# Two-expert outputs: weighting on ScalarE, adding on GpSimd, and a later place for the last normalisation steps

## The reference

```python
    # 2: sparse experts, two for each token
    out = out + w_e[:, None] * h
    # 3: learned adjacency, mixed with the layer norm of x
    return (1.0 - gamma) * adj_raw + gamma * A_learned
    # 4: transformer block
    h = _rmsnorm(hidden_states, ln1_w)
    q = (h @ Wq); k = (h @ Wk); v = (h @ Wv)
```

## Time and profile before

| what | value |
|---|---|
| median of 3 runs | 1102.59 us (1101.93 to 1104.66) |
| the profiled execution's own time | 1102.88 us |
| its span (what the profile covers) | 1101.0 us |
| PE busy | 1006.5 us, 91% |
| DVE busy | 868.8 us, 79% |
| ACT busy | 613.7 us, 56% |
| POOL busy | 430.9 us, 39% |

### The profile page before, as it was taken

The page is one execution under the profiler, slowest core; times in us unless marked ns, Lnnn a source line. Parts: engine busy times, 40 slices in busy tenths (PEclk is TensorE's granted clock), DMA queues, the critical chain, the costliest instruction groups (busy, mean ns, idle before and its releaser), DMA issues.

```text
span 1101.0 us, 20158 instructions
## 1 busy us (share of the span) xinstructions
PE 1006.5 (91%) x5934; PEld 821.6 (75%) x5934; DVE 868.8 (79%) x2642; ACT 613.7 (56%) x1748; POOL 430.9 (39%) x372
## 2 busy tenths in 40 slices
PE   4788877999996489999999999999998999999997
PEld 2455545466663368999999999999887888888886
DVE  6999996577773889878777877777868888788877
ACT  4789983533232377777787777777952222222231
POOL 5798892633321233323332333222422232233231
PEclk9968887699998699999999999999999999999999
DMA  9700003011113111010101000000011111111111
GB/s 286 257 1 2 1 2 110 27 47 49 44 39 117 60 39 49 1 39 2 49 1 40 13 23 1 2 1 1 15 30 29 44 43 52 48 43 44 56 43 38
DMA packets 49459, 49.25 MB, mean 45 GB/s; under 512 B 4896, under 2 KB 42464, under 8 KB 49376
## 3 DMA queue, kind: packets, MB, share of 16 engines
q1 hardware_dynamic: 45888, 40.83, 11.8%
q0 software_dynamic: 2208, 6.03, 1.8%
q10 hardware_dynamic: 1280, 1.38, 0.5%
HBM read 43.11 MB, written 5.11 MB: 44 GB/s over the span
## 4 chain that ended last, share of the span: by engine, by line
PE 71%; DVE 12%; ACT 7%; POOL 5%; issue 4%; DMA 1%; SPq 0%; DVEq 0%; ACTq 0%; POOLq 0%
PE bank L57 13%; PE bank L58 13%; PE bank L59 13%; PE bank L957 6%; PE bank L978 4%; PE bank L852 4%; PE bank L860 4%; PE bank L879 4%; PE bank L967 3%; PE bank L979 2%; POOL rest L1418 2%; POOL alpha L1421 1%; DVE alpha L1626 1%; ACT alpha L1069 1%; ACT alpha L1054 1%
## 5 line engine op out<-in xcount | busy, mean ns | idle before, releaser
L1483 POOL TENSOR_TENSOR rot_s<-swap,rq 128x512 f32<-128x512 f32 x64 | 88.5, 1384 | 194.7 <-ACT swap L1261 194.6
L1137 ACT ACTIVATE silu<-bank 128x512 f32<-128x512 f32 x66 | 39.4, 598 | 173.6 <-PE bank L59 173.6
L2066 DVE TENSOR_TENSOR o_ring<-bank,o_ring 128x256 fp32r<-128x256 f32 x128 | 54.2, 424 | 80.2 <-ACT o_ring L1290 78.7
L1274 ACT ACTIVATE prob<-prob,pmin 128x128 f32<-128x128 f32 (+1 forms) x256 | 113.3, 447 | 5.4 <-DVE pmin L2047 5.4
L957 PE MATMUL bank<-kv,norm 128*128 128x128 f32 (+1 forms) x512 | 106.1, 330 | 6.1 <-DVE norm L2040 5.9
L1889 DVE SCALAR_TENSOR_TENSOR xs<-bank,wt,xs 128x256 f32<-128x256 f32 x264 | 109.0, 476 | 0.1
L1439 POOL TENSOR_TENSOR gate_r<-gate_w,gate_r 128x256 fp32r<-128x256 f32 x31 | 36.4, 1175 | 177.3 <-ACT gate_r L1130 177.3
L1290 ACT ACTIVATE o_ring<-bank 128x256 fp32r<-128x256 f32 x128 | 48.3, 378 | 76.4 <-PE bank L979 76.3
L57 PE MATMUL bank<-wo_r,o_ring 128*128 128x256 f32 x256 | 82.5, 322 | 0.0
L1867 DVE TENSOR_TENSOR hidf<-silu,bank 128x512 f32<-128x512 f32 x66 | 45.4, 688 | 44.9 <-ACT silu L1137 43.2
L2059 DVE TENSOR_SCALAR prob<-prob,pinv 128x128 f32<-128x128 f32 (+1 forms) x256 | 76.9, 343 | 4.6
(11 more groups left out here) (304 smaller groups left out, 3087.0 us busy)
## 6 DMA issues: line engine op xcount, KB each, us to landing
gate_w<-in_Wg SPq DMA_DIRECT2D x33, 128.0 KB, 2.1
up_w<-in_Wu SPq DMA_DIRECT2D x33, 128.0 KB, 2.3
down_w<-in_Wd SPq DMA_DIRECT2D x33, 128.0 KB, 2.3
w_all<-in_w_gate SPq DMA_DIRECT2D x8, 512.0 KB, 10.5
w_all<-in_w_up SPq DMA_DIRECT2D x8, 512.0 KB, 10.3
w_all<-in_w_down SPq DMA_DIRECT2D x8, 512.0 KB, 10.6
wq_g<-in_Wq SPq DMA_DIRECT2D x4, 1024.0 KB, 5.8
wo_g<-in_Wo SPq DMA_DIRECT2D x4, 1024.0 KB, 5.5
```

The source lines that it names most:

```text
L1274: ins = act.activation(prob[:, u % 4, nt * P:nt * P + (nt + 1) * P], prob[:, u % 4, nt * P:nt * P + (nt + 1) * P], ACT.Exp, bias=pmin[:, u ...
L1483: pool.tensor_tensor(rot_s[:, m % 2].rearrange("p (b n) -> p b n", b=2), swap[:, m % 2].rearrange("p (b n) -> p b n", b=2), bcast(tab[:, 1 ...
```

## The change

Tiles 3 to 7 (`BY_POOL`) are no longer gathered by VectorE. ScalarE multiplies `ytok` by the token's weights in place (`weigh_rows`, two activations a tile), GpSimd adds both into `xs` (`add_rows`, two additions a tile). The loads of expert rank 1 are issued by ScalarE instead of SyncE. The split of the activations is handed over for columns 0 to 255 (half of half 0) and 512 to 1023 (half 1): ScalarE writes the high part, GpSimd the low one. Columns 256 to 511 stay with VectorE. `measure(2)` moves ahead of `normalise_rows(1)`, and `measure(b)` for b of 1 to 3 waits until GpSimd has added the rows. In the loop, VectorE's `mix_learned(2)`, `normalise_rows(2)`, `mix_learned(3)` and `normalise_rows(3)` come one to two steps later, behind the copy of the values and the cosines of the keys, with ScalarE's roots and the transposes moved to fit.

```diff
+        BY_POOL = range(3, T)
@@ SyncE
             for b in range(B):
-                for k in range(K0):
-                    rows = y_rows[(k * T + NT * b) * P:(k * T + NT * b + NT) * P, :]
-                    sp.dma_start(ytok[:, k, NT * b:NT * b + NT, :], rows.rearrange("(u p) c -> p u c", p=P)
-                                 ).then_inc(S[f"tok_in{b}"], 16)
+                sp.dma_start(ytok[:, 0, NT * b:NT * b + NT, :], y_of(b, 0)).then_inc(S[f"tok_in{b}"], 16)
@@ TensorE, attention
-                    for t in {-1: (4, 5), 1: (6, 7)}.get(k, ()):
+                    for t in {0: (4, 5), 2: (6, 7)}.get(k, ()):
                         turn_rows_norm(t)
@@ ScalarE
+            def weigh_rows(t):
+                act.wait_ge(S[f"tok_in{t // NT}"], 16 * K0)
+                for k in range(K0):
+                    act.activation(ytok[:, k, t, :], ytok[:, k, t, :], ACT.Copy, scale=w_tok[:, k, t:t + 1]
+                                   ).then_inc(S["y_scaled"], 1)
+            def high_activations(cols):
+                act.wait_ge(S["normT_copied"], T + cols.stop // P)
+                act.activation(actT_r[:, 0, :, cols], actT[:, :, cols], ACT.Copy).then_inc(S["actT_hi"], 1)
@@ ScalarE, attention
-                    if k == -6:
+                    if k == -5:
                         roots_out(2)
-                    if k == -4:
+                    if k == -3:
                         roots_in(3)
-                    if k == -1:
+                    if k == 0:
                         roots_out(3)
-                    for t in {0: (4, 5), 2: (6, 7)}.get(k, ()):
+                    for t in {1: (4, 5), 3: (6, 7)}.get(k, ()):
                         scaled_copy(1, t, turn_bank(t))
+                    if k == 4:
+                        high_activations(slice(512, 1024))
@@ ScalarE, ahead of the attention
+            for par in range(3):
+                act.wait_ge(S[f"y_out{par}"], 16 * len(range(par, TILES, 3)))
+            for b in range(B):
+                act.dma_start(ytok[:, 1, NT * b:NT * b + NT, :], y_of(b, 1)).then_inc(S[f"tok_in{b}"], 16)
+            weigh_rows(3)
             roots_in(0)
+            weigh_rows(4)
             roots_out(0)
             roots_in(1)
             for t in range(NT):
                 scaled_copy(1, t, turn_bank(t))
+            high_activations(slice(0, 256))
+            weigh_rows(5)
             roots_out(1)
             for t in range(NT, 2 * NT):
                 scaled_copy(1, t, turn_bank(t))
+            weigh_rows(6)
+            weigh_rows(7)
@@ GpSimd
+            def add_rows(t):
+                n = K0 * (t - BY_POOL.start)
+                for k in range(K0):
+                    pool.wait_ge(S["y_scaled"], n + k + 1)
+                    if k >= 1:
+                        pool.wait_ge(S["y_added"], n + k)
+                    pool.tensor_tensor(xs[:, t, :], xs[:, t, :], ytok[:, k, t, :], ALU.add).then_inc(S["y_added"], 1)
+            def low_activations(cols, count):
+                pool.wait_ge(S["actT_hi"], count)
+                pool.tensor_tensor(actT_r[:, 1, :, cols], actT[:, :, cols], actT_r[:, 0, :, cols].bitcast(F32),
+                                   ALU.subtract).then_inc(S["actT_lo"], 1)
...
+            add_rows(3)
+            add_rows(4)
+            low_activations(slice(0, 256), 1)
+            for t in range(5, T):
+                add_rows(t)
             pool.wait_ge(S["att_in"], 48)
             for k in range(FIRST, END):
+                if k == 4:
+                    low_activations(slice(512, 1024), 3)
@@ VectorE
             def measure(b):
+                if b >= 1:
+                    dve.wait_ge(S["y_added"], K0 * (NT * b + NT - BY_POOL.start))
@@ VectorE, into_attention
                 mix_learned(0)
-                gather(3)
                 measure(1)
                 normalise_rows(0)
                 mix_learned(1)
-                split_activations(1, slice(0, 256), 1)
+                measure(2)
                 normalise_rows(1)
-                gather(4)
                 split_activations(1, slice(256, 512), 2)
-                gather(5)
-                measure(2)
@@ VectorE, attention
-                    if k == -7:
+                    if k == -6:
                         mix_learned(2)
-                    if k == -6:
-                        gather(6)
                     if k == -5:
-                        gather(7)
-                    if k == -4:
                         measure(3)
+                    if k == -2:
                         normalise_rows(2)
-                    if k == -2:
+                    if k == -1:
                         mix_learned(3)
-                    if k == -1:
+                    if k == 1:
                         normalise_rows(3)
-                    if k == 3:
-                        split_activations(1, slice(512, 1024), 3)
```

More of the change, by code:

```diff
@@ L325, in build @@
             "norm_done", "normT_ready", "normT_copied",
-            "aT_ready", "aT_used", "tok_var", "tok_sd", "x3_var", "x3_sd",
+            "aT_ready", "aT_used", "tok_var", "tok_sd", "x3_var", "x3_sd", "y_scaled", "y_added",
             "logit_ready", "rexp_done", "rmax_done", "sq_done", "ms_done", "rms_done", "norm2_done", "norm2T_ready", "x3_added",
@@ L386, in build, with y_of @@
         BLOCKS = 2 * KV
+        BY_POOL = range(3, T)
+        def y_of(b, k):
+            return y_rows[(k * T + NT * b) * P:(k * T + NT * b + NT) * P, :].rearrange("(u p) c -> p u c", p=P)
         BU = 2 * REP
```

## The result

The changed kernel takes 1105.99 us (median of 20 runs, 1105.16 to 1109.39) where the kernel before took 1103.47 in the same comparison (20 runs, 1101.85 to 1107.61). The ratio is 1.0024 [1.0016, 1.0031]: slower by 2.5 us. That lies within the 0.3% that I had called no change, but the interval excludes a gain, and the forecast was a gain of 0.3 us. The direction was wrong, and the sum behind it fell short by 2.8 us.

A forecast was written before the change was run, and what follows sets the result against it. VectorE mostly sets the pace up to the full softmax loop, ScalarE from 390 to 400 us. ScalarE 0.85 early and VectorE 0.3 late gave 0.3 us gained: profiled 1102.88 becomes 1102.6, median forecast 1102.3 us, range 1098.4 to 1106.0.

The forecast's parts named there:

- First part: Loading to first key matmul: VectorE idles 2.7 us at measure(2) for tile 5; keys 3.4 us behind.
- Second part: First key matmul to first shift: rotated keys level, first scores 4.3 us earlier, shift(0) 2.1 us earlier.
- Third part: ScalarE from shift(0) to high_out(2): table loads and roots net +1.85, split -1.7, high part +1.1; 0.85 us early.
- The Exp load lies in the wait for `shift(0)`: ScalarE before the first softmax unit: the Exp table load is hidden by waiting, saving 1.28 us.
- rival 3: ScalarE empties before each table load, so a switch costs more than its load: 2.6 us late, 1104.9; chance 0.04.
- Fourth part: VectorE up to low_out(2): normalise(4) held 1.4 us, and about 0.4 more behind another low part; 0.3 us late.
- taken the middle: At high_out(2) and low_out(2): between ScalarE 0.85 early and VectorE 0.3 late, 0.3 us gained.
- Behind that a shift is simply carried to the end: After about 410 us, with the softmax loop in full flow, any gain or loss stays unchanged to the end.
- Rival 1: GpSimd's pieces slip between VectorE's instructions: shift(0) at 385.2, both engines 3.9 us early, 1098.7 us; chance 0.24.
- Rival 2: Wait for tile 5 grows: stage 1 4.2 us or more late, shift(0) at 390.5 or later, 1106.5 us; chance 0.16.

The follow-up runs named there:

- tile5_first: Changed kernel with tile 5 weighted and added ahead of the first split: 1103.29 us, ratio 0.9995 to the kernel before.
- roots_first: Changed kernel with the last pair of square roots, roots_out(3), ahead of the first exponential: 1103.62 us, ratio 0.9999 to the kernel before.
- group 4: Four more profiles, two of each unmodified kernel: 1106.24 and 1104.59 us after, 1103.38 and 1104.94 before; its table sets clock drops against seam lengths.
- handover_only: Changed kernel with the loop order of before and measure(2) behind the split again; weighting, adding and splits stay handed over: 1105.52 us, ratio 1.0018.

## Why the prediction failed in its sum and held in most of its steps

**First part, right.** The wait at `measure(2)` was put at 2.7 us and is 2.73; the keys 3.4 us behind, measured 2.9. The weightings take 0.50 each, 0.89 for a pair, where I took 0.40 each; the additions 0.72 and the 128x512 low part 1.27 as taken. `tile5_first` shows what the wait is worth: 2.5 us of the seam. I had the wait and its chain right and did not draw the conclusion that it would be carried to the end almost in full.

**Second part, right but for one milestone.** Values, rotated keys and `shift(0)` lie 0.2 to 0.9 us from the forecast, all on the early side. The first scores (383.37) are 1.5 us later than forecast: the addition of query 0's rotation, at 381.65, took 1.67 us instead of 0.69 beside GpSimd's sines. `shift(0)` did not suffer from it.

**Third part, the first failed step.** "The Exp load lies in the wait for `shift(0)`" is wrong. ScalarE did not wait for `shift(0)`, which started at 387.90: it came from the swap of a query that TensorE had projected just before (387.25 and 387.85, after 5.31 us of waiting for TensorE), and the load followed at 388.46. The load is paid as before, so the balance of ScalarE is 7.94 - 4.71 = 3.23 us and not 1.85. The 2.9 us won up to `shift(0)` are all gone at the swap, and `roots_first` gives back 2.7 of them. That the swap is even so only 0.4 later than forecast is luck: the balance was 1.4 too good, and the load started 3.1 us earlier than before where I had counted on 2.1. The price of a switch in this order was right; rival 3 falls, since activations stand directly ahead of and behind each load (391.28 to 392.57, 393.07 to 394.37). The Trainium skill (ScalarE: Activation LUTs, What ACT_TABLE_LOAD costs) adds a drain of about 1380 ns to each load; the trace and the 2.68 us for two switches disagree with it.

**Fourth part, the failed step that decided the sign.** ScalarE stood 0.45 us early at `high_out(2)` (0.85 forecast), VectorE 0.1 late at `low_out(2)` (0.3 forecast). I had closed the account there and "taken the middle". But `shift(6)`, just ahead of it on VectorE, was already 0.73 late, and `low_out(2)` hid that only because VectorE had waited 0.56 us for ScalarE there before. The next `normalise` was held for another 1.09, by sines that ScalarE's lead of 0.45 had brought forward. With VectorE at 98% from there, its lag alone is carried on, and ScalarE's lead bought nothing: +0.84 at `shift(10)`, +0.86 at `shift(40)`, where the forecast had -0.3. That is the error of 1.2 us in the seam.

**Not foreseen, 1.5 us behind the seam.** "Behind that a shift is simply carried to the end" holds up to 830 us, where the clock drop adds 1.5. It came at the seam lengths of the table in group 4, whatever the kernel; why just at those is open. It is the larger part of the measured difference: 0.9 + 1.5 = 2.4, against 2.5 in the medians.

**The rivals.** Rival 1 (cheap locks) falls with the holds in `handover_only` and at 406.73. Rival 2 has its first half (the wait) but not its condition: `shift(0)` came at 387.90, well ahead of 390; the loss has another way, over the table loads. Its time of 1106.5 is near the measured one for the wrong reason.

## What to carry to other kernels

Work taken off the busiest engine is worth nothing while something else ends last at each milestone: price the waits and the table loads on the receiving engines first. Place an activation of another table where its engine idles, and ahead of the first use of the next table, and check by the trace what the engine does just before, for a load hides in a wait only if there is one. Where two engines feed one full loop, take the later one, not the mean, and follow it for some units past the first milestone that happens to agree. And a lead on one engine is not only good: it moves the start of the next engine's work, which can then fall on an instruction that had been free.

## What the hardware showed that I had not expected

A VectorE instruction between SBUF operands of the kinds used here (`TENSOR_SCALAR`, `TENSOR_TENSOR`, `SCALAR_TENSOR_TENSOR`), however small, can stand until the running GpSimd instruction ends: 1.31 us for a `TENSOR_SCALAR` on 128x2 (0.22 elsewhere), 1.96 us for the pair of `normalise` (0.55) beside a GpSimd instruction of 2.38 us. Those that read PSUM run at their usual time beside it (0.69 us for the cosines at 388.47 and 0.42 for the `shift` at 389.29 in the changed kernel, beside sines from 388.52 to 389.79), and so does `BATCH_NORM_STATS2` (0.75 for the pair at 354.52, beside additions from 354.44 to 356.03).

The granted clock of TensorE near 830 us was 0.66 in the changed kernel and 1.00 in the one before, with equal work and some 400 us behind the last difference between them; it comes to 1.5 us. It came and went with the length of a stretch 400 us earlier, and none of these runs explains why.
